# Query projection in seven block products in place of eight, with attention ordered by token half, key head and pair

## What is computed

```python
q = (hidden_states @ Wq.T).reshape(b, s, H, D).transpose(0, 2, 1, 3)
...
scores = jnp.einsum('bhqd,bhkd->bhqk', q, k) * scale
...
attn = jax.nn.softmax(scores, axis=-1)
out = jnp.einsum('bhqk,bhkd->bhqd', attn, v)
out = out.transpose(0, 2, 1, 3).reshape(b, s, H * D)
return out @ Wo.T
```

## Time and profile before

| | |
|---|---|
| median of 3 runs | 1754.7 us (1750.4 to 1756.32) |
| the profiled execution: time | 1754.61 us |
| the profiled execution: span of the trace | 1752.8 us |
| granted clock, mean | 0.992 |
| PE, DVE, ACT, POOL busy | 97%, 50%, 44%, 17% |

### The profile page before, as it was taken

One profiled execution on the slowest core, in us unless ns is written; L12 is line 12 of the kernel. 1 busy time (PEld: TensorE's weight loads), 2 busy tenths in 40 slices (PEclk: granted clock), 3 DMA queues, 4 the chain that ended last, 5 costly groups with the idle time before them and its releaser, 6 DMA issues. The chain is left out here.

```text
span 1752.8 us, 25373 instructions
## 1 busy us (share of the span) xinstructions
PE 1696.2 (97%) x8546; PEld 1427.7 (81%) x8546; DVE 871.8 (50%) x2683; ACT 778.8 (44%) x2143; POOL 298.5 (17%) x669
## 2 busy tenths in 40 slices
PE   5888999999999999999999999999999999999999
PEld 4667897888888888888888888888888788888887
DVE  7776010555555555555556546556566553323212
ACT  4476434555455455445445536545545432121111
POOL 4611000221131122122112113112222000000000
PEclk9989999999999999999999999999999999999999
DMA  5200425111111101101101101100100231000000
GB/s 158 72 1 1 156 80 208 37 25 37 37 25 36 37 24 38 37 13 49 37 13 49 37 13 41 38 20 17 45 13 19 80 95 43 1 24 1 24 1 24
DMA packets 47001, 74.73 MB, mean 43 GB/s; under 512 B 4576, under 2 KB 23008, under 8 KB 44832
## 3 DMA queue, kind: packets, MB, share of 16 engines
q1 hardware_dynamic: 45984, 72.63, 13.0%
q10 hardware_dynamic: 896, 0.56, 0.1%
HBM read 52.20 MB, written 20.97 MB: 42 GB/s over the span
## 5 line engine op out<-in xcount | busy, mean ns | idle before, releaser
L961 POOL TENSOR_SCALAR prob<-prob,inv_sum 128x128 f32<-128x128 f32 x256 | 98.5, 385 | 829.3 <-DVE inv_sum L1104 829.3
L1199 PE MATMUL ps_q<-h_hi,kv_w_hi 128*128 128x512 f32 x512 | 205.7, 402 | 1.4 <-PEq L758 1.4
L989 ACT ACTIVATE prob<-prob,neg_max 128x128 f32<-128x128 f32 x256 | 100.7, 393 | 238.4 <-DVE neg_max L1099 238.4
L1199 PE MATMUL ps_q<-h_lo,kv_w_hi 128*128 128x512 f32 x512 | 200.1, 391 | 0.0
L1199 PE MATMUL ps_q<-h_hi,kv_w_lo 128*128 128x512 f32 x512 | 199.8, 390 | 0.0
L133 ACT ACTIVATE prob_t_hi<-ps_s 128x512 fp32r<-128x512 f32 x192 | 107.4, 598 | 73.9 <-PE ps_s L1248 73.9
L962 POOL TENSOR_SCALAR prob<-prob,inv_sum 128x256 f32<-128x256 f32 x256 | 136.9, 535 | 0.0
L1084 DVE TENSOR_TENSOR x<-ps_q,x 128x512 f32<-128x512 f32 x128 | 88.3, 690 | 97.6 <-PE ps_q L1277 97.6
L138 DVE TENSOR_TENSOR prob_t_lo<-ps_s,prob_t_hi 128x512 fp32r<-128x512 f32 x192 | 126.2, 685 | 15.1 <-ACT prob_t_hi L133 12.5
L1466 DVE SCALAR_TENSOR_TENSOR f_act<-f_ps_r,f_scale,f_act 128x512 f32<-128x512 f32 x44 | 33.0, 751 | 192.1 <-PE f_ps_r L1497 190.7
L991 ACT ACTIVATE prob<-prob,neg_max 128x256 f32<-128x256 f32 x256 | 127.2, 497 | 0.0
(11 more groups left out here) (184 smaller groups left out, 4244.8 us busy)
## 6 DMA issues: line engine op xcount, KB each, us to landing
k_scratch<-kv_stage SPq DMA_DIRECT2D x32, 256.0 KB, 2.4
v_scratch<-kv_stage SPq DMA_DIRECT2D x32, 256.0 KB, 2.0
w_raw<-in_wq_g SPq DMA_DIRECT2D x8, 1024.0 KB, 4.8
k_raw<-k_scratch SPq DMA_DIRECT2D x32, 256.0 KB, 3.5
v_raw<-v_scratch SPq DMA_DIRECT2D x32, 256.0 KB, 4.0
w_raw<-in_wo_g SPq DMA_DIRECT2D x8, 1024.0 KB, 6.2
x<-in_x SPq DMA_DIRECT2D x16, 256.0 KB, 2.9
out<-x SPq DMA_DIRECT2D x16, 256.0 KB, 2.1
```

The costliest lines, as they stand in the source:

```text
L961: pool.tensor_scalar(prob[:, b, h, 0:P], prob[:, b, h, 0:P], inv_sum[:, b, h, 0:1], 1.0, ALU.mult, ALU.mult)
L989: act.activation(prob[:, b, h, 0:P], prob[:, b, h, 0:P], ACT.Exp, scale=-1.0, bias=neg_max[:, b, h, 0:1], accum_out=row_sum[:, b, h, 0:1])
L1199: last = pe.matmul(ps_q[:, h % 2, :], wq[a][:, c, h * HEAD:(h + 1) * HEAD], h3[b][:, c, pair * PAIR:(pair + 1) * PAIR], start=(c == 0 and ...
```

## The change

The query projection of one key head (4 heads, 512 rows of weights) for a half of the tokens (two pairs, 1024 tokens) is taken as a product of 2 x 2 blocks: the weights A in blocks of two heads by two channel chunks, the tokens B in blocks of two chunks by one pair. It is computed as seven block products P1 to P7 of sums of blocks, and the result's four blocks are sums of those. A block product is two halves i = 0, 1 (one head each) of 6 matmuls, one half to each bank of `ps_q`.

```diff
+FACTORS = {"P1": ("A11", "B11"), "P2": ("A12", "B21"), "P3": ("S4", "B22"), "P4": ("A22", "T4"), "P5": ("S1", "T1"), "P6": ("S2", "T2"), "P7": ("S3", "T3")}
+TOKEN_OPERANDS = ("B11", "T2", "B21", "T3", "T4", "T1", "B22")
...
+    def made_lo_part(self, pool, name, n):
+        pool.wait_ge(self.made_hi, self.count(name, n))
+        lo_part(pool, [w[:, :, :] for w in self.operand(name)], self.block(name)).then_inc(self.made_lo, 1)
+
+    def make(self, pool, n):
+
+        pool.wait_ge(self.given_lo, self.count("A22", n))
+        pool.tensor_tensor(self.block("S1"), self.block("A21"), self.block("A22"), ALU.add).then_inc(self.made, 1)
+        pool.wait_ge(self.given_lo, self.count("A11", n))
+        pool.wait_ge(self.made, 4 * n + 1)
+        pool.tensor_tensor(self.block("S3"), self.block("A11"), self.block("A21"), ALU.subtract).then_inc(self.made, 1)
+        pool.wait_ge(self.made, 4 * n + 2)
+        pool.tensor_tensor(self.block("S2"), self.block("S1"), self.block("A11"), ALU.subtract).then_inc(self.made, 1)
+        pool.wait_ge(self.given_lo, self.count("A12", n))
+        pool.wait_ge(self.made, 4 * n + 3)
+        pool.tensor_tensor(self.block("S4"), self.block("A12"), self.block("S2"), ALU.subtract).then_inc(self.made, 1)
+        self.made_lo_part(pool, "S2", n)
+        self.made_lo_part(pool, "S3", n)
...
+                def copy(i, n):
+
+                    act.wait_ge(q_done, weights.products("P1", i, n))
+                    act.wait_ge(weights.made_lo, weights.count("S3", n))
+                    act.activation(partial[i].rearrange("p b t n -> p b (t n)"), ps_q[:, i, :].rearrange("p (b n) -> p b n", b=2), ACT.Copy).then_inc(q_copied, 1)
...
+                def total(name, i, n):
+
+                    product, part = {"U2": ("P6", partial), "C11": ("P2", partial), "U3": ("P7", second), "C21": ("P4", third),
+                                     "C22": ("P5", third), "U4": ("P5", second), "C12": ("P3", second)}[name]
+                    dve.wait_ge(q_done, weights.products(product, i, n))
+                    by_tile = ps_q[:, i, :].rearrange("p (b t n) -> p b t n", b=2, t=2)
+                    dve.tensor_tensor(held[name][i][:, :, :, :], by_tile, part[i][:, :, :, :], ALU.add).then_inc(q_summed, 1)
...
+                def product(name, i, n):
+
+                    a, b = FACTORS[name]
+                    left, right = weights.operand(a), operands.operand(b)
+                    weights.await_operand(pe, a, n)
+                    if n == KV_HEADS:
+                        operands.await_loaded(pe, b)
+                    if name == "P6":
+                        pe.wait_ge(q_copied, 2 * n + i + 1)
+                    elif name in ("P2", "P7", "P4", "P3"):
+                        pe.wait_ge(q_summed, summed({"P2": "U2", "P7": "C11", "P4": "U3", "P3": "U4"}[name], i, n))
+                    elif name == "P5" and n == 0:
+                        pe.wait_ge(q_summed, summed("C21", i, n))
+                    for c in range(2):
+                        for m, (s, t) in enumerate(PASSES):
+                            done = pe.matmul(ps_q[:, i, :], left[s][:, c, i * HEAD:(i + 1) * HEAD], right[t][:, c, :],
+                                             start=(c == 0 and m == 0), stop=(c == 1 and m == 2))
+                    done.then_inc(q_done, 1)
...
+                def first_pair(u, n):
+
+                    scores(u, 0)
+                    if u:
+                        output(u - 1, 1, 1)
+                        pe.wait_ge(y_read, 4 * u - 1)
+                    product("P5", 0, n)
+                    scores(u, 1)
+                    if u:
+                        pe.wait_ge(y_read, 4 * u)
+                    product("P5", 1, n)
+                    flip(u, 0, 0)
+                    flip(u, 0, 1)
+                    product("P3", 0, n)
+                    flip(u, 0, 2)
+                    product("P3", 1, n)
+                    values(u, 0, 0)
+                    values(u, 0, 1)
+                    second_half(u)
+                    if n + 1 < SETS:
+                        output(u, 1, 0)
+                        output(u, 1, 1)
+
+                def second_pair(u, n):
+
+                    scores(u, 0)
+                    pe.wait_ge(y_read, 4 * u - 1)
+                    product("P1", 0, n + 1)
+                    pe.wait_ge(y_read, 4 * u)
+                    product("P1", 1, n + 1)
+                    scores(u, 1)
+                    product("P6", 0, n + 1)
+                    product("P6", 1, n + 1)
+                    flip(u, 0, 0)
+                    flip(u, 0, 1)
+                    product("P2", 0, n + 1)
+                    flip(u, 0, 2)
+                    product("P2", 1, n + 1)
+                    product("P7", 0, n + 1)
+                    values(u, 0, 0)
+                    product("P7", 1, n + 1)
+                    values(u, 0, 1)
+                    product("P4", 0, n + 1)
+                    product("P4", 1, n + 1)
+                    second_half(u)
+                    output(u, 1, 0)
```

More of the change, by code:

```diff
@@ L897, in attention @@
         ps_o = ps("ps_o", [P, 2, HID], st)
+        partial = [weights.block(room).rearrange("p b (t n) -> p b t n", t=2) for room in ("S2", "S3")]
+        second = [sb(f"q_second_part{i}", [P, 2, 2, P], F32, st) for i in range(2)]
+        third = [sb(f"q_third_part{i}", [P, 2, 2, P], F32, st) for i in range(2)]
+        held = {"C11": partial, "C21": partial, "U2": second, "U4": second, "C12": second, "U3": third, "C22": third}
         k_loaded, v_loaded = sem("k_loaded"), sem("v_loaded")
+        wo_hi, wo_lo = weights.wo_hi, weights.wo_lo
         mask_zero, mask_done = sem("mask_zero"), sem("mask_done")
@@ new lines, in query_lo, with prob_lo, out_lo @@
+                def query_lo(name, i, n):
+                    dve.wait_ge(q_hi, read(name, i, n))
+                    lo_part(dve, [w[:, head(name, i), :, :] for w in q_second], held[name][i][:, :, 1, :]).then_inc(q_read, 1)
+                def prob_lo(u, b, blk):
+                    dve.wait_ge(t_hi, 6 * u + 3 * b + blk + 1)
+                    lo_part(dve, [w[blk] for w in prob_t], ps_t[:, (b + blk) % 2, :]).then_inc(t_lo, 1)
+                def out_lo(u, b, half):
+                    dve.wait_ge(o_hi, 4 * u + 2 * b + half + 1)
+                    lo_part(dve, [w[:, half, :, :].rearrange("p h n -> p (h n)") for w in o[b]], ps_o[:, half, :]).then_inc(o_lo, 1)
@@ L1193, in _ @@
+                for u in range(UNITS):
+                    if u == UNITS - 1:
+                        last_pair(u)
+                    elif u % 2:
+                        second_pair(u, u // 2)
+                    else:
+                        first_pair(u, u // 2)
             @block.tensor
             def _(pe):
[L1195 to L1201 removed]
@@ new lines, in scores, with flip @@
+                        done.then_inc(s_done, 1)
+                def flip(u, b, blk):
+                    n = 6 * u + 3 * b + blk
+                    if blk == 0:
+                        pe.wait_ge(normed, HEADS * u + GROUP * (b + 1))
+                    if b == 0 and blk < 2:
+                        pe.wait_ge(scored, HEADS * u + GROUP + 3 + blk)
+                    else:
+                        pe.wait_ge(t_lo, n - 1)
+                    for h in range(GROUP):
+                        done = pe.transpose(ps_t[:, (b + blk) % 2, h * P:(h + 1) * P], prob[:, b, h, blk * P:(blk + 1) * P], ident[:, :])
+                    done.then_inc(t_done, 1)
@@ new lines, in values @@
+                def values(u, b, half):
+                    if b == 0 and half == 0:
+                        pe.wait_ge(v_lo, u + 1)
+                    if not (u == 0 and b == 0):
+                        pe.wait_ge(o_lo, 4 * u + 2 * b - 1 + half)
+                    blocks = (((0, 0),), ((1, 0), (2, 1)))[half]
+                    for n, (blk, tile) in enumerate(blocks):
+                        pe.wait_ge(t_lo, 6 * u + 3 * b + blk + 1)
+                        for m, (i, j) in enumerate(PASSES):
+                            done = pe.matmul(ps_o[:, half, :], v[i][:, 2 * b + tile, :], prob_t[j][blk],
+                                             start=(n == 0 and m == 0), stop=(n == len(blocks) - 1 and m == 2))
+                    done.then_inc(pv_done, 1)
@@ new lines, in output @@
+                def output(u, b, half):
+                    if b == 0 and half == 0 and u % 2 == 0:
+                        pe.wait_ge(wo_lo, GROUP * (u // 2) + GROUP)
+                    if b:
+                        pe.wait_ge(y_read, 4 * u + 1 + half)
+                    elif u == UNITS - 1:
+                        pe.wait_ge(feed.h_lo, 3 + half)
+                    elif u % 2:
+                        pe.wait_ge(q_summed, summed("C21", half, u // 2 + 1))
+                    else:
+                        pe.wait_ge(q_summed, summed("C12", half, u // 2))
+                    pe.wait_ge(o_lo, 4 * u + 2 * b + half + 1)
```

(17 more changed lines are left out.)

953 lines of the change are left out of this document (570 added, 383 removed).

## The result

The changed kernel takes **1733.45 us** (median of four runs, 1728.99 to 1734.37), the kernel before 1754.63; the ratio is **0.988**, 95% interval 0.985 to 0.990. I had said 1722 us in a range of 1707 to 1742, chance of faster 0.91. The gain is real and two thirds of what I summed: 21 us in place of 32. The profiled execution has a span of 1732.2 us against 1752.8.

The account below looks back on a forecast made before the run. PE, busy 97% of the span, was taken as the bound. From 1754.6 us, -43.5 for matmuls and +3.9, +1.6, +5.6 and +0.4 for waits gave 1722.6, stated as 1722 us, range 1707 to 1742.

Parts of the forecast that it names:

- Matmuls: Attention's query projection: 192 fewer 512-column matmuls at a pitch of 0.227 us each, -43.5 us.
- Rival C: Query matmuls worth their busy time, 0.394 us each, with few waits: gain 75.6 us, time 1690 us, chance 0.03.
- P1's second half: Odd pairs: PE waits 0.26 us for DVE's residual add before this half, 15 times, +3.9 us.
- U4: Even pairs: PE waits 0.1 us for this DVE sum before P3's second half, 16 times, +1.6 us.
- Collision of POOL and DVE: Even pair's end: they exclude each other, delaying PE's last output; between 0 and 11.2 us, middle taken, +5.6 us.
- The waits before transposes: PE's old waits in attention, 4.1 us; kept in the sum, dropped only for the range's 1707 us.
- low end: The range's fastest time: matmuls alone give 1711 us, and without the old 4.1 us of waits 1707 us.
- Start of attention: Before the first scores: last product summed, copied and lowered in 2.3 us against 1.99, +0.4 us.
- Keys and values: Stage before attention: added sums, copies, lows and stores are covered, zero cost; up to 10 us if cover fails.
- if the stage from 205 to 297 grows: Sign that the forecast is wrong: the key and value stage before attention becoming longer.
- POOL's tensor-tensor takes over 1.6 us: Sign that the forecast is wrong: such POOL operations in attention exceeding 1.6 us, against 1.29 in the first stage.

Follow-up runs that it names:

- extra_mm: Changed kernel plus one overwritten 512-column matmul ahead of ten of fourteen product halves per key head from the second on, 150 in all: 1761.82 us, ratio 1.005.
- add_first: Changed kernel with DVE's residual add ahead of its four scores in the odd pair: 1725.26 us, ratio 0.984.
- best: Changed kernel with earlier residual add and output lowering, layer-norm statistics and last normalizations in gaps, layer-norm tiles in their old place: 1713.27 us, ratio 0.975.
- after_again: The changed kernel run once more, nothing edited: 1731.58 us, ratio 0.988.
- ln_place: Changed kernel with the tiles of three layer norms back in their old SBUF place: 1728.62 us, ratio 0.986.
- before_moved: Kernel before with only the three layer norms' tiles moved as the change does, 1056 bytes lower for h3, kv_w and w_raw: 1755.47 us, ratio 1.0003.
- shift32: Changed kernel with 32 unused SBUF bytes ahead of h3, shifting h3, kv_w, w_raw and the latents: 1731.13 us, ratio 0.987.
- pad32: Changed kernel with 32 unused SBUF bytes behind the moved layer norms, shifting the latents while h3 and kv_w stay: 1731.48 us, ratio 0.988.
- given_order: Changed kernel with DVE lowering the even pair's second-half attention output before the third given weight block, not after: 1725.94 us, ratio 0.984.
- pool_late: Changed kernel with POOL starting its four weight-block sums only after DVE has lowered the third given block: 1726.97 us, ratio 0.985.

## Why the prediction was right, and where its sum was short

Right: faster, and by the forecast's mechanism; no rival's. The profiled run lies 11.4 us above the sum (1734.0 against 1722.6), and the median still inside the forecast's own 1707 to 1735. That is partly luck: misses of some 15 us upwards, most of them in places that I had given no term, and of 4 downwards stood against each other. Point by point:

1. **Matmuls, -43.5.** Right: 1344 query matmuls at the pitch; extra_mm prices one at 0.223 to 0.225 us. Rival C is out.
2. **P1's second half, +3.9.** Mechanism and place right; by add_first it is 5.3. The wait is 0.23 of my 0.26 us; what failed is that I priced only the wait, not the 0.11 us in which PE gets going again.
3. **U4, +1.6.** P3's first half with its transposes behind it: the transposes take 0.46 us there and 0.35 elsewhere, 0.11 x 16 = 1.8. The sum U4 ends just then (721.18 us in one even pair, PE goes on at 721.33); no run took it away, so that the 0.1 us is this wait is argued.
4. **Collision of POOL and DVE, +5.6** (the middle between 0 and 0.75 us). Measured 0.38 a set, 5.7 us. That POOL lengthens DVE's lows was right, the figure luck: a middle between two cases, of which the second, "if POOL gets one turn", is what happened (2.99 - 1.89 = 1.10 us). I had priced it at 0.75, but PE had 0.75 us of room for it; a low alone takes 0.63 us, not my 0.69.
5. **The waits before transposes, 4.1 us.** I kept them in the sum and let them go only in the low end. They went, all but 0.6. With 2 to 4 this gives a set of 65.13, where 64.5 and my waits of 0.26, 0.1 and 0.375 make 65.2: right to a tenth, partly since this and the restarts cancel.
6. **Start of attention, +0.4.** 2.14 us of idle against 1.99, and 16.20 us from first product to scores against 13.16, 2.72 of it for twelve matmuls: +0.3. My own figures (2.3 against 1.99) gave 0.3 too.
7. **Keys and values, 0.** This is the step that failed first. The cover that I argued for held: with the layer norms in their place the stage ends where it did, sums and stores included. But I costed the tiles' move, one line of the diff, at nothing, and it costs 2.45 us. My tripwire "if the stage from 205 to 297 grows" caught it; the cause was none that I had named.
8. **The ends of the loop.** The sum was steady state times 15 or 16 and treated units 29 to 31 like the rest. The statistics now stand ahead of a sum that PE waits for (1.8 us, of which the kernel before lost 0.9 in the same unit, 34.34 against 33.42: +0.9), the normalizations ahead of the last scores (+3.6 in the last unit, 1.7 of it by the lower clock), and PE's wait for `up_lo` at the feed-forward's start grew from 2.0 to 3.3 us. That makes 5.8 us, the largest part of the miss. Why the last grew wasn't tried. It is there in every changed kernel (3.2 to 3.3 us) and is the first load of `f_raw`: issued 0.19 us behind the feed-forward's first matmul in both kernels, it lands after 4.54 us, before after 3.29.
9. **The last outputs' pace.** 5.60 us for 24 matmuls without a wait, 5.46 before: 0.14 x 15 = 2.1 us. `o1` lies in another place than before; that this is the cause is not shown, and with the layer norms back in their place (best) it is 5.60 us as well.
10. **POOL.** "Wrong if POOL's tensor-tensor takes over 1.6 us": the sum of S1 does, 1.65 on average, but only that one of fourteen, all others being at 1.3 to 1.56, and 3.0 us of cover take it up. As a threshold it was set without asking how many of the chain would pass it.

The misses in sum: P1 and U4 +1.6, collision +0.1, waits before transposes -3.5, start -0.1, place +2.5, outputs' pace +2.1, the ends +5.8, and what one execution lost with the clock, 1.8 ahead of the keys and 0.9 in unit 0 (31.31 us, 30.42 in after_again): +11.2 of 11.4.

## What to carry to other kernels

Sum a steady loop by a laid-out timeline, as here, and then cost its last two turns by themselves: what is hooked in there (the next stage's statistics, its first loads) meets the new order at its worst, and the stall of 1.8 us there came with a granted clock of 0.50 in ten of the eleven kernels that have it (1.7 us in the changed one). Price a wait of PE at more than its length: here 0.23 us cost 0.11 more. When DVE and POOL both read two SBUF tensors, start POOL's operations when DVE's urgent ones are done: three lows took 1.89 us in place of 2.99, and one wait condition was worth 5.7 us. And list what a change moves in memory: an allocation that moves is an edit, here one of 2.45 us.

## What the runs showed of the hardware that I hadn't expected

- Unbroken matmuls of 512 columns followed each other at different paces. In the key and value stage it was 0.2267 us before and in ln_place, 0.2333 in before_moved, after_again and shift32, and in pad32 0.229 for keys and 0.2333 for values: it switched when only the operands' SBUF addresses were changed. Addresses are not all of it: the last output of an even pair goes on at 0.229 us where it comes after a wait (changed kernel, add_first), and at 0.2333, with the same operands in the same place, where the wait is gone (given_order, pool_late).
- DVE and POOL lengthened each other's operations where DVE had two SBUF inputs: three lows 1.89 us alone, 2.99 beside POOL, and POOL 1.29 alone, 1.67 beside DVE. With DVE reading PSUM neither grew (0.69 and 1.29 us side by side, pool_late).
- PE's idles of about 2 us came with a fall of the granted clock from 1.00 to 0.50 in some executions and not in others; what decides isn't shown. At the first scores the changed kernel idles 2.14 us (the row `kv_w_lo` above), and the clock is then 0.50 for some 3 us (unit 0 takes 31.31 us); in after_again it stays at 1.00 around an idle of 2.15 us at the same place (30.42 us), and so it does around one of 1.81 us in the first unit of best. In the last unit, around an idle of 1.8 to 1.9 us, it fell in ten of the eleven kernels that have this stall, for 3 to 7 us, and not in shift32. Such a fall is 1.7 us in the changed kernel's last unit and 0.9 in its first: as much as some of the differences between these kernels, so that those are read from sets and stretches and not from medians.
